# A gated state-space layer and expert FFN: seven units for five, GpSimd products in pairs, thinner TensorE matmuls

## What is computed

```python
x = x + tanh(g_xattn) * ssm(ctx, layernorm(x))
x = x + tanh(g_ffn) * ffn(layernorm(x))

def ssm(h, z):
    xc = conv4(in_proj_w @ h); u = silu(xc + conv_b)          # 512 channels
    dt_lo, B, C = split(x_proj_w @ u)                         # 16, 16, 16 rows
    delta = softplus(dt_proj_w @ dt_lo + dt_proj_b)
    state = state * exp(delta * A) + (delta * u) * B          # 512 channels x 16 states, token by token
    y = sum_n(state * C) + D * u
    return y * silu(z)

def ffn(x):
    probs = softmax(x @ gate_w.T); rw, sel = top2(probs); rw /= rw.sum()
    h = gelu(x @ wd + bd) * combine                           # eight experts of 128
    return h @ wu + combine @ bu + gelu(x @ ws_d + bs_d) @ ws_u + bs_u
```

## Time and profile before

| | us |
|---|---|
| median of three runs | 680.33 (677.32 to 680.44) |
| the profiled execution, its own time | 678.83 |
| its span, first to last instruction | 677.1 |
| GpSimd busy, 278 instructions | 496.7 |
| VectorE busy, 556 | 509.2 |
| TensorE busy, 1772 | 508.2 |
| ScalarE busy, 594 | 347.6 |

### The profile page before, as it was taken

One profiled execution on the slowest core, in us unless ns is written; L12 is line 12 of the kernel. 1 busy time (PEld: TensorE's weight loads), 2 busy tenths in 40 slices (PEclk: granted clock), 3 DMA queues, 4 the chain that ended last, 5 costly groups with the idle time before them and its releaser, 6 DMA issues.

```text
span 677.1 us, 6131 instructions
## 1 busy us (share of the span) xinstructions
PE 508.2 (75%) x1772; PEld 223.8 (33%) x1772; DVE 509.2 (75%) x556; ACT 347.6 (51%) x594; POOL 496.7 (73%) x278
## 2 busy tenths in 40 slices
PE   5377242323366998797979979787998999998998
PEld 2022010101022333232423423243343344676676
DVE  3553889787889977899999989997688899614311
ACT  2277533343425698634676575533968734265300
POOL 3026999999998969999999999985588969300000
PEclk9586566767588997897999998979898889999799
DMA  8676513031373304234664120263341321200011
GB/s 258 256 255 252 188 58 125 33 122 62 125 248 125 111 25 148 93 117 154 235 213 154 48 78 32 93 233 140 111 135 53 109 74 52 77 1 1 0 55 54
DMA packets 35325, 79.61 MB, mean 118 GB/s; under 512 B 5497, under 2 KB 9145, under 8 KB 35292
## 3 DMA queue, kind: packets, MB, share of 16 engines
q1 hardware_dynamic: 35292, 79.22, 33.8%
HBM read 62.17 MB, written 17.04 MB: 117 GB/s over the span
## 4 chain that ended last, share of the span: by engine, by line
POOL 29%; PE 25%; DVE 19%; issue 18%; ACT 7%; DMA 2%; POOLq 0%; SPq 0%; ACTq 0%; DVEq 0%
POOL ring L834 16%; POOL ring L843 10%; PE wk L1348 10%; DVE decay L1040 5%; PE wk L1334 5%; DVE ring L1040 5%; PE y_ps L1273 4%; PE wk L1289 2%; ACT decay L899 1%; PE wk L1310 1%; DMA b_in<-bc_scratch 1%; POOL dd_out L816 1%; DVE h L1221 1%; DVE ring L1060 1%; ACT h L986 1%
## 5 line engine op out<-in xcount | busy, mean ns | idle before, releaser
L834 POOL TENSOR_TENSOR ring<-dd,b_in 128x1024 f32<-128x1024 f32 x128 | 299.1, 2354 | 13.9 <-DMA dd<-dd_scratch 10.4
L899 ACT ACTIVATE decay<-dd,a_neg 128x511 f32<-128x511 f32 (+2 forms) x320 | 176.5, 590 | 64.2 <-DVE ring L1040 35.1
L843 POOL TENSOR_TENSOR ring<-ring,c_in 128x1024 f32<-128x1024 f32 x64 | 150.4, 2351 | 25.9 <-DVE carry L1052 16.1
L1273 PE MATMUL y_ps<-ring,fold 128*32 128x512 f32 (+1 forms) x640 | 86.0, 677 | 99.4 <-POOL ring L843 97.2
L1040 DVE TENSOR_TENSOR_SCAN ring<-decay,ring 128x1024 f32<-128x1024 f32 x56 | 127.0, 2280 | 20.1 <-ACT decay L899 13.6
L1040 DVE TENSOR_TENSOR_SCAN decay<-decay,ring 128x1024 f32<-128x1024 f32 x56 | 128.0, 2286 | 15.1 <-ACT decay L899 15.1
L1334 PE MATMUL wk<-xc,w_down 128*128 128x512 f32 (+1 forms) x360 | 134.1, 526 | 4.5 <-issue 4.4
L1348 PE MATMUL wk<-h,w_up 128*128 128x512 f32 (+1 forms) x360 | 132.3, 523 | 0.0
L1334 PEld LDWEIGHTS wk<-xc,w_down 128*128 128x128 f32 x360 | 68.0, 194 | 66.8 <-issue 60.8
L1348 PEld LDWEIGHTS wk<-h,w_up 128*128 128x128 f32 x360 | 68.8, 196 | 54.2 <-issue 49.3
L1060 DVE TENSOR_TENSOR ring<-decay,c_in 128x1024 f32<-128x1024 f32 x64 | 78.4, 1225 | 6.7
(11 more groups left out here) (97 smaller groups left out, 441.1 us busy)
## 6 DMA issues: line engine op xcount, KB each, us to landing
dd<-dd_scratch SPq DMA_DIRECT2D x48, 512.0 KB, 3.8
dd<-dd_scratch SPq DMA_DIRECT2D x32, 256.0 KB, 2.9
dd_scratch<-dd_out SPq DMA_DIRECT2D x12, 512.0 KB, 2.9
z<-in_x SPq DMA_DIRECT2D x4, 1024.0 KB, 6.2
x<-in_xT SPq DMA_DIRECT2D x4, 1024.0 KB, 5.8
c_in<-bc_scratch SPq DMA_DIRECT2D x8, 512.0 KB, 4.9
b_in<-bc_scratch SPq DMA_DIRECT2D x8, 512.0 KB, 5.0
x_scratch<-x SPq DMA_DIRECT2D x3, 1024.0 KB, 8.7
```

The costliest lines, as they stand in the source:

```text
L834: nc.gpsimd.tensor_tensor(ring[:, i % RING].rearrange("p (q n) -> p q n", n=n), dd[:, j % DD_RING, None, n:2 * n].broadcast_to([P, TILES[v ...
L843: nc.gpsimd.tensor_tensor(ring[:, i % RING], ring[:, i % RING], c_in[:, g % BC_RING], ALU.mult).then_inc(weighed_pool, 1)
L899: last = nc.scalar.activation(decay[:, i % 2, q * n + first:(q + 1) * n], dd[:, j % DD_RING, first:n], ACT.Exp, scale=a_neg[:, c, r, k:k + 1])
L1273: last = nc.tensor.matmul(y_ps[r * BLOCK:(r + 1) * BLOCK, 0:n], fold[:], ring[:, slots[r] % RING, q * n:(q + 1) * n], start=False, stop=p ...
```

## The change

UNITS now has batches 0, 1 and 3 in halves and batch 2 whole: seven units, of which 1, 3 and 6 are second halves. GpSimd makes the products of two neighbouring slots in one instruction (`outers`) and weighs the first two slots of a group in one, which now stands at times of its own in PLAN ("weigh"). For a first half it first copies the last columns of both slots to carry; the two slots that VectorE weighs keep their copies on VectorE. On TensorE, d_diag becomes four 32 by 32 diagonals on four quarters of the rows and columns. Mean, variance and gate logits become four matmuls of 32 columns, each to its own quarter of the partitions; ScalarE copies the four partial sums (`evacuate_sums`) and one more matmul adds them. RING is 10, AHEAD 4, DD_OUT 3. z and x of batch 0 leave `first_loads` and stand in PLAN, as do bias and weight loads, between the loads of dd. PLAN has new numbers throughout.

```diff
-UNITS = [(0, 0, 512), (1, 0, 512), (2, 0, 512), (3, 0, 256), (3, 256, 256)]
+UNITS = [(0, 0, 256), (0, 256, 256), (1, 0, 256), (1, 256, 256), (2, 0, 512), (3, 0, 256), (3, 256, 256)]
-RING = 9
+RING = 10
-DD_OUT = 4
+DD_OUT = 3
-AHEAD = 3
+AHEAD = 4
-POOL_WEIGHS = (1, 2)
+POOL_WEIGHS = (0, 1)
...
     "load_ffn": [
-        [-12.75, -11.61, -11.52, -11.43, -11.35, -11.26, -11.17, -11.08, -11, -10.91, -10.82],
+        [-1.56, -0.34, 0.17, 0.5, 1.89, 2.32, 4.07, 4.53, 5.39, 5.6, 6.79],
...
-        d_diag = sb("d_diag", [P, NW, P])
+        d_diag = sb("d_diag", [P, NW, BLOCK])
-        mean_w = one_of_dm.broadcast_to([P, P])
+        mean_w = one_of_dm.broadcast_to([P, BLOCK])
+        group_w = one_of_block.broadcast_to([P, P])
...
-            def outer(i):
+            def outers(i):
...
+                for k in (j, j + 1):
+                    pool.wait_ge(dd_loaded[k % DD_RING], DMA * (k // DD_RING + 1))
                 pool.wait_ge(b_loaded[g % BC_RING], DMA * (g // BC_RING + 1))
                 if i >= RING:
-                    pool.wait_ge(summed, (i - RING) // NR4 + 1)
+                    pool.wait_ge(summed, (i + 1 - RING) // NR4 + 1)
+                nc.gpsimd.tensor_tensor(ring[:, i % RING:i % RING + 2].rearrange("p s (q n) -> p s q n", n=n),
+                                        dd[:, j % DD_RING:j % DD_RING + 2, None, n:2 * n].broadcast_to([P, 2, TILES[v], n]),
+                                        b_in[:, None, g % BC_RING].rearrange("p o (q n) -> p o q n", n=n).broadcast_to([P, 2, TILES[v], n]),
+                                        ALU.mult).then_inc(outer_ready, 2)
             def weigh(i):
...
+                if goes_on(v):
+                    j, k = c * NR4 + r, p * TILES[v]
+                    nc.gpsimd.tensor_copy(carry[:, j - 1:j + 1, k:k + TILES[v], None],
+                                          two.rearrange("p s (q n) -> p s q n", n=n)[:, :, :, n - 1:n]).then_inc(carried, 1)
...
+                nc.gpsimd.tensor_tensor(two, two, c_in[:, None, g % BC_RING].broadcast_to([P, 2, WIDE]),
+                                        ALU.mult).then_inc(weighed_pool, 2)
...
-                if slot + AHEAD < START[NU]:
-                    outer(slot + AHEAD)
-                if slot >= 0 and weighs_on_pool(slot):
-                    weigh(slot)
+                if slot + AHEAD < START[NU] and (slot + AHEAD) % 2 == 0:
+                    outers(slot + AHEAD)
...
-                    nc.tensor.matmul(y_ps[:, 0:n], d_diag[:, c, :], u[:, w % U_RING, 0:n], start=True, stop=False)
+                    for r in range(NR4):
+                        rows = slice(r * BLOCK, (r + 1) * BLOCK)
+                        nc.tensor.matmul(y_ps[rows, 0:n], d_diag[rows, c, :], u[rows, w % U_RING, 0:n], start=True, stop=False)
...
-                if name == "mean":
+                if name == "mean_p":
                     for j in range(NW):
                         pe.wait_ge(x2_ready, NW * v + j + 1)
-                        last = nc.tensor.matmul(o, mean_w, x2[:, j, cols], start=j == 0, stop=j == NW - 1)
+                        last = nc.tensor.matmul(o[j * BLOCK:(j + 1) * BLOCK, :], mean_w, x2[:, j, cols], start=True, stop=True)
...
+                if name in ("mean", "var"):
+                    wait_drained(pe, name + "_p", v)
+                    last = nc.tensor.matmul(o, group_w, part_sum[:, 0:n], start=True, stop=True)
```

More of the change, by code:

```diff
@@ L103, in weighs, with carries @@
     return sum(weighs_on_pool(j) == pool for j in range(i))
+def carries(i):
+    v, c, p, r = PLACES[i]
+    k = ((p + 1) * TILES[v] - 1) // TILES[v - 1]
+    return sum(goes_on(PLACES[j][0]) and j % NR4 == POOL_WEIGHS[1] for j in range(slot_of(v - 1, c, k, NR4 - 1) + 1))
 def block_no(v, c, r):
@@ L152 @@
     ],
     "mean": [
-        [34.29],
-        [67.9],
-        [98.26],
-        [116.84],
-        [132],
+        [26.67],
+        [34.15],
+        [51.96],
+        [69.34],
+        [98.17],
+        [117.04],
+        [132.13],
+    ],
+    "var_p": [
+        [27.55],
+        [44.27],
+        [57.75],
+        [76.5],
+        [99.05],
+        [123.24],
+        [133.1],
     ],
     "var": [
-        [36.53],
-        [72.92],
-        [102.77],
-        [130.39],
-        [133.48],
+        [27.85],
+        [45.16],
+        [59.67],
+        [77.04],
+        [99.3],
+        [123.45],
+        [133.4],
@@ L338 @@
-        [2.2, 2.4, 2.6, 2.8],
-        [53.2, 53.4, 53.6, 53.8],
-        [77.2, 77.4, 77.6, 77.8],
-        [105.5, 105.75, 106.25, 106.5],
+        [0.667, 0.75, 0.833, 0.917],
+        [11.25, 11.5, 11.75, 13.333],
+        [25.333, 25.667, 26.5, 27.25],
+        [43.25, 43.5, 43.75, 45.25],
+        [56.25, 56.5, 56.75, 59.333],
+        [89.25, 89.5, 89.75, 91.333],
+        [112.6, 112.7, 112.8, 112.9],
+    ],
+    "mean_p read": [
+        [27.75],
+        [35.667],
+        [53.75],
+        [71.4],
+        [100.5],
+        [116.5],
+        [128.387],
@@ L342 @@
     ],
     "square": [
-        [38.5],
-        [74.333],
-        [103.5],
-        [128.03],
-        [128.121],
+        [29.333],
+        [36.833],
+        [55.333],
+        [71.8],
+        [101.25],
+        [124.5],
+        [128.452],
+    ],
+    "var_p read": [
+        [29.667],
+        [45.75],
+        [59.667],
+        [78.5],
+        [101.5],
+        [125.333],
+        [128.484],
     ],
     "var read": [
-        [39.5],
-        [76.5],
-        [105.25],
-        [128.061],
@@ L476, in by_slot @@
     return due
-JOBS = ("in_proj", "x_proj", "dt", "mean", "var", "lg_t", "lg", "comb", "down", "mix", "up")
+JOBS = ("in_proj", "x_proj", "dt", "mean_p", "mean", "var_p", "var", "lg_t", "lg", "comb", "down", "mix", "up")
 PE_ORDER = in_order("y", *JOBS)
 SP_ORDER = in_order("ctx", "z", "x", "xdbl", "dd", "load_dd", "load_b", "load_c", "load_ffn", "x2_store", "x_out", "out")
-POOL_DUE = by_slot("affine_z", "du", "residual")
-ACT_DUE = by_slot("in_proj read", "silu", "x_proj read", "dt read", "square", "var read", "lg_t read", "share_exp",
+POOL_DUE = by_slot("affine_z", "du", "residual", "weigh")
+ACT_DUE = by_slot("in_proj read", "silu", "x_proj read", "dt read", "mean_p read", "square", "var_p read", "var read", "lg_t read", "share_exp",
                   "comb read", "down read", "gelu")
@@ L530, in mamba_moe_kernel @@
         rank = sb("rank", [P, NX])
-        consts = sb("consts", [P, 7])
-        gates = consts[:, 5:7]
-        eps, minus_half, minus_one, one_of_dm, one = (consts[:, k:k + 1] for k in range(5))
-        mean_w = one_of_dm.broadcast_to([P, P])
+        consts = sb("consts", [P, 8])
+        gates = consts[:, 6:8]
+        eps, minus_half, minus_one, one_of_dm, one, one_of_block = (consts[:, k:k + 1] for k in range(6))
+        mean_w = one_of_dm.broadcast_to([P, BLOCK])
+        group_w = one_of_block.broadcast_to([P, P])
         zeros = sb("zeros", [P, STATES, 1])
@@ L1005, in what_is_due @@
                             exp_tables()
+                    if name == "mean_p read":
+                        evacuate_sums("mean_p", v)
+                    if name == "var_p read":
+                        evacuate_sums("var_p", v)
                     if name == "square":
@@ L1046, in scan @@
                                                             carry[:, j, k:k + 1], ALU.mult, ALU.add)
-                if goes_on(v):
+                if goes_on(v) and not weighs_on_pool(i):
                     steps[0] += 1
@@ L1315, in job @@
                     for j in range(NW):
-                        last = nc.tensor.matmul(o[0:NX, :], gate_w[:, j, :], xc[:, j, cols], start=j == 0, stop=j == NW - 1)
+                        last = nc.tensor.matmul(o[j * BLOCK:(j + 1) * BLOCK, :], gate_w[:, j, :], xc[:, j, cols], start=True, stop=True)
                 if name == "lg":
```

518 lines of the change are left out of this document (321 added, 197 removed), and 68 rows, old and new, of the table PLAN.

## The result

| | before | after |
|---|---|---|
| median (us) | 679.09 (677.32 to 680.44) | 686.82 (685.77 to 687.95) |
| span of the profiled execution | 677.1 | 686.0 |

The ratio is 1.0116, with a 95% interval of 1.0081 to 1.015, four runs each. The forecast was 665 us, between 641 and 684. "Slower" had a chance of 0.12 in it, for a reason that turned out not to be the one.

The account below looks back on a forecast made before the run. GpSimd and VectorE shared the bound, and the change would make VectorE the fuller. Start 35.5, VectorE's work 512, stall 7, idle 42 and tail 66.5 made 663, so 665 us with 1.7 outside the span; range 641 to 684.

Parts of the forecast that it names:

- The start: Up to the first scan: first pair of products at 31 us, first scan at 35.5, 30.5 ahead of the old steady flow.
- GpSimd, ScalarE, VectorE's work: Busy totals: GpSimd some 490 us with pairs about 4.53, ScalarE about 420, VectorE 538, of which 512 in the middle.
- the stall is between 0 and 13.6; I take 7, the middle: Bias split on VectorE in slot 6, beside GpSimd's pairs of 4.5 us: its waiting for them adds 7 us.
- With VectorE the fuller engine these 22 go. I keep 42: VectorE's idle time in the middle, 64 us before: waits for y (15.6) and products (6.5) vanish, 42 stay.
- one engine that sets the pace of the whole middle: First scan to last y: VectorE, busy for 512 us against GpSimd's 482, is the fuller engine and sets the time.
- The last y: End of the middle: the last y comes 5 us after VectorE's last scan, as before, despite down ahead of it.
- down that delays the last y by over 5: Listed sign of being wrong: down jobs ahead of the last y on TensorE hold it up by over 5 us.
- The tail: From the last y to the end: 66.5 us where it was 88.8, one down and the holes around routing gone.
- The sum: Whole execution: 35.5 + 512 + 7 + 42 = 596.5, with the tail's 66.5 a span of 663, so 665 us.
- The second: Rival on TensorE: row tiles sharing a PSUM bank go one after another, +5 us in the last unit, 670; chance 0.1.
- The third: Rival: ScalarE takes GpSimd's place, each of six unit changes stalls VectorE 3.7 us more, 687 us; chance 0.12.
- where over 35 were needed: Listed sign of being wrong: VectorE's scans wait for decay from ScalarE above 35 us in total.

Follow-up runs that it names:

- e7: e1 with z of batch 0 and its statistics earlier and the first c load behind the first three dd loads; 668.35 us, ratio 0.983.
- e1: The changed kernel with the 13 small bias loads ahead of the x_dbl store and the bias split ahead of the first scan; 669.94 us, ratio 0.986.
- e2: The changed kernel with the last y behind four of the nine down jobs instead of behind all nine; 688.78 us, ratio 1.0155.
- e13: e1 with one unused VectorE reduction of 256 columns more behind every slot's scan, 34.0 us of busy time; 687.52 us.
- e8: e1 with the last y earlier and its gate on VectorE ahead of the routing; 666.03 us, ratio 0.9803.
- e14: e1 with one unused ScalarE copy of 128 columns more behind every slot's exponentials, 27.0 us of busy time; 668.51 us.

## Why the prediction was wrong

**The start, +2.7 us.** First pair at 33.7 instead of 31, first scan at 38.2 instead of 35.5. I had priced the store and the load of dd by the median of all dd loads. Here b and c, a megabyte, are issued just ahead of the store, and the first dd load could be issued only 6.4 us after the store. In e7, with c behind, it was 3.9 us (5.6 in e1), and the first pair came at 31.1.

**GpSimd, ScalarE, VectorE's work: right.** A pair takes 4.54 us, and the totals of GpSimd and ScalarE are within 1%. VectorE's work from the first scan to the last y is 517.7 + 2.5 - 12.4 = 507.8 us, where 512 was forecast.

**The step that turned the verdict: "the stall is between 0 and 13.6; I take 7, the middle".** It measured 12.4, +5.4 on the sum. The row that decided was there, a copy of 170 to 2008 ns, and the middle between two ends is no argument when one end has a mechanism. The Trainium skill, SBUF — State Buffer, section Who interferes with whom, had the lock held for a whole instruction, and by that rule the sum was 7 higher. Here the trace agrees: 4.87 us for each of three instructions beside pairs, 0.69 to 0.74 beside nothing. The casts and the tensor_scalar ran beside GpSimd's small instructions in this trace. e2's has one cast beside a weighing of a pair, and it took 4.60 us instead of 0.44: the cast pays too, and 12.4 is what this execution paid, not a fixed price. Whether the tensor_scalar is spared no run tells.

Also missed was a choice and no size. I took the split's place as given and counted its 4.4 us of work into the 512. Stall and work together are 16.8 us by the trace, and e1 measured 16.9 for the move. That is more than the 7.7 us by which the change is slower: without it the verdict is the one forecast, 669.9, inside the range. This is the part of the account that an experiment shows.

**The largest miss, "With VectorE the fuller engine these 22 go. I keep 42": +13.6 us.** From the first scan to the last y VectorE was idle for 575.8 - 520.2 = 55.6. Who it waited for there:

```profile
DVE logit L1349 <- PE wk L1514: 6.2, 1, 6.2
DVE decay L1226 <- ACT decay L1073: 6.0, 3, 4.2
DVE x_out L1414 <- PE wk L1542: 5.8, 4, 3.5
DVE decay L1233 <- ACT decay L1073: 4.7, 3, 3.5
DVE y_gated L1285 <- PE y_ps L1463: 4.6, 3, 2.0
DVE second L1387 <- ACT share L1149: 4.5, 1, 4.5
```

The first scan's own wait ends at 38.2 and isn't counted. The waits for y fell from 15.6 to 4.6, and those for products from 6.5 to nothing: 17.5 of the 22 went. The waits of the scans for ScalarE, which I had let stay, fell too, from 21.3 to 14.3. But others came or grew. The wait for the logits is 6.2 us, most of the time between the last weighing and the last y. Those of x_out are 5.8, and those of second rose from 1.6 to 4.5. The gaps for which the trace names nobody rose from 9.0 to 13.7 us, with 689 instructions instead of 443. I had taken 22 from the 64 as if nothing could take their place. That is read off one trace; no run here takes one of these waits away by itself. The model behind it, one engine that sets the pace of the whole middle, is wrong too. In e1 GpSimd is full up to 150 us, and behind that a little over half of VectorE's added work lands (e13); the rest goes into its short waits.

**The last y: 8.5 us instead of 5.** The list of what would show me wrong had "down that delays the last y by over 5". It did, and that is 3.5 of the 13.6. But putting the y earlier gained nothing, in e2 or in e8, since TensorE has the same work either way.

**The tail, +5.5 us.** The work is as counted. The granted clock fell twice, which I had not priced. TensorE's stretches of the tail:

```profile
614.00:623.00 9.00, 6.31 (x34) 1.94 (x24) 6.20 (x21) 4.22 (x8) 0.72 (x1) 0.73 0.17 58
623.00:631.00 8.00, 8.00 (x30) 5.61 (x30) 1.71 (x2) 1.04 (x3) 0.00 (x0) 0.66 0.01 2
631.00:663.00 32.00, 31.38 (x144) 24.95 (x142) 7.60 (x33) 12.54 (x19) 0.00 (x0) 0.99 0.09 29
663.00:671.00 8.00, 7.70 (x21) 5.97 (x22) 0.64 (x2) 0.00 (x0) 0.00 (x0) 0.60 0.06 17
```

The two up jobs lose 2.33 and 2.97 us, 5.3 together: nearly the whole miss. The first fall is in every trace of this order, the second in some only, so 3 of the 5.5 us are the luck of the profiled execution.

**The sum.** 2.7 + 5.4 - 4.2 + 13.6 + 5.5 = 23.0, from 663 to the span of 686.0.

**The rivals.** The second (row tiles one after another) is out: the four d_diag pieces of a half start within 0.02 us of each other and take 0.63 us together, where one piece of full width took about 0.6. The Trainium skill's rule (TensorEngine Tiling (Array Packing), section Restrictions and Gotchas) that different row tiles can't access one PSUM bank at once isn't borne out by this row, for tiles that write different partitions of the bank. The third named the right time, 687, for the wrong reason: VectorE's waits for ScalarE at its scans are 14.3 us (6.0, 4.7 and 3.6) where over 35 were needed. That decides it; e14, which adds 27 us to ScalarE for nothing, agrees.

## What to carry to other kernels

When a change moves work out of a stretch in which an engine stood idle, cost the move itself: what the work takes there, what it meets there, and whether the move could be left out. A VectorE instruction with two inputs in SBUF, placed beside long GpSimd instructions, cost the length of one of them here, and a cast once did. Such work belongs where GpSimd rests, and longer GpSimd instructions raise that price. Before a small gain is counted on an engine, ask whether it is the full one in that very stretch.
